# Keys times v left in PSUM for its scan, the first scan in mid-pass, and fourteen list writes a pass in new places on GpSimd's queue

## What is computed

```python
x = x + attn(layernorm(x)); x = x + moe(layernorm(x))

# attn
q, k, v = split(x @ w_qkv);  q, k = elu(q) + 1, elu(k) + 1
running_kv   = scan(k * v, decay)      # s_t = decay * s_(t-1) + x_t, per channel
running_ksum = scan(k, decay)
den = clip(sum(q * running_ksum, per head), 1e-6)
out = (q * running_kv / den) @ w_out

# moe
top_vals, top_idx = top_k(x @ router_w.T + router_b, 4)
rw = softmax(top_vals) * 1.8
routed = sum over the 4 of rw * down_e(silu(gate_e(x)) * up_e(x));  out = routed + shared(x)
```

## Time and profile before

| | us |
|---|---|
| three runs, median (lowest to highest) | 662.66 (661.18 to 666.01) |
| the profiled execution | 662.23 |
| its span, from its first to its last instruction | 660.5 |
| nine steps of the loop, the last of them over at about | 236 |
| 191 tiles, up to about | 596 |

### The profile page before, as it was taken

How to read it: one execution, slowest core, us unless ns; L and a number is a source line. 1 busy time by engine, 2 the same in 40 slices (tenths; PEclk the granted TensorE clock), 3 DMA queues, 4 the chain that set the end, 5 groups by cost and what they waited for, 6 DMA issues and landing times.

```text
span 660.5 us, 15988 instructions
## 1 busy us (share of the span) xinstructions
PE 578.3 (88%) x4909; PEld 409.2 (62%) x4909; DVE 479.9 (73%) x1907; ACT 471.1 (71%) x1138; POOL 438.2 (66%) x359
## 2 busy tenths in 40 slices
PE   4899999899898979999999999999999999998000
PEld 2476676476575557777777777777777777775000
DVE  3569999899979887776666666666666666665163
ACT  4778887769776458897888888788888888787000
POOL 3033177888888877752888888788888788788100
PEclk9999999899999999999999999999999999999555
DMA  8945687879786799976888888898998888886799
GB/s 332 337 147 181 223 261 247 285 265 328 242 265 209 263 288 307 341 265 178 146 141 146 142 143 140 141 147 136 147 146 143 143 140 142 140 140 75 251 409 381
DMA packets 102070, 140.43 MB, mean 213 GB/s; under 512 B 15522, under 2 KB 87746, under 8 KB 101442
## 3 DMA queue, kind: packets, MB, share of 16 engines
q1 hardware_dynamic: 69424, 97.28, 45.9%
q0 software_dynamic: 29040, 38.68, 34.7%
q10 hardware_dynamic: 3522, 3.44, 1.7%
HBM read 79.19 MB, written 64.89 MB: 218 GB/s over the span
## 4 chain that ended last, share of the span: by engine, by line
PE 53%; POOL 13%; DVE 9%; issue 9%; DMA 9%; SPq 3%; ACT 3%; POOLq 0%; ACTq 0%; DVEq 0%
PE psD L1356 13%; PE psQ L1325 12%; PE psK L1325 12%; POOL xlist_scratch L589 8%; PE psT L1296 5%; DMA acc_scratch<-arena 5%; SPq L518 3%; DMA W<-acc_scratch 2%; PE psT L1347 2%; PE psV L1347 2%; PE psD L1413 2%; POOL rstd L574 2%; POOL W L567 1%; POOL acc_scratch L636 1%; DVE stats L843 1%
## 5 line engine op out<-in xcount | busy, mean ns | idle before, releaser
L636 POOL DMA_INDIRECT acc_scratch<-arena x159 | 250.5, 1575 | 72.7 <-ACT arena L692 37.9
L589 POOL DMA_INDIRECT xlist_scratch<-list_row,dest x128 | 136.9, 1069 | 38.6 <-issue 35.9
L1356 PE MATMUL psD<-W,arena 128*128 (+1 forms) x955 | 135.5, 273 | 0.0
L1141 DVE COPY arena<-psT 128x512 f16<-128x512 f16 x191 | 81.0, 424 | 67.2 <-PE psT L1296 65.6
L1325 PE MATMUL psK<-W,arena 128*128 (+1 forms) x576 | 109.3, 326 | 0.7 <-DVE arena L1141 0.7
L1325 PE MATMUL psQ<-W,arena 128*128 (+1 forms) x570 | 108.2, 326 | 0.1
L1356 PEld LDWEIGHTS psD<-W,arena 128*128 128x128 f16 x955 | 85.4, 98 | 6.8 <-ACT arena L680 0.3
L683 ACT ACTIVATE arena<-arena 128x192 f16<-128x192 f32 x191 | 69.2, 362 | 12.0 <-DVE arena L1163 0.6
L692 ACT ACTIVATE arena<-psD,arena 128x256 f32<-128x256 f32 x159 | 73.1, 459 | 6.3 <-DMA acc_scratch<-arena 5.8
L1296 PEld LDWEIGHTS psT<-ident,arena 128*128 128x128 f16 x764 | 58.0, 98 | 25.9 <-issue 2.1
L1296 PE MATMUL psT<-ident,arena 128*128 128x128 f16 x764 | 73.9, 219 | 0.0
(11 more groups left out here) (185 smaller groups left out, 1085.9 us busy)
## 6 DMA issues: line engine op xcount, KB each, us to landing
arena<-xlist_scratch SPq DMA_DIRECT2D x159, 136.0 KB
arena<-in_w_early_dram SPq DMA_DIRECT2D x24, 640.0 KB, 4.9
W<-acc_scratch SPq DMA_DIRECT2D x24, 512.0 KB, 12.6
acc_scratch<-arena SPq DMA_DIRECT2D x16, 512.0 KB, 8.9
arena<-in_L_attn_x_dram SPq DMA_DIRECT2D x10, 512.0 KB, 5.8
xlist_scratch<-pad_scratch SPq DMA_DIRECT2D x32, 136.0 KB
list_row<-xrow_scratch SPq DMA_DIRECT2D x32, 136.0 KB
acc_scratch<-arena SPq DMA_DIRECT2D x33, 128.0 KB, 15.2
```

What stands on the lines that cost most here:

```text
L589: nc.gpsimd.indirect_dma_start(xlist[:, :], bass.IndirectOffsetOnAxis(ap=dest[:, n:n + 1], axis=0), list_row[j % LISTS][:, :], None).then_ ...
L636: nc.gpsimd.indirect_dma_start(acc[t % ACCS][:, :], bass.IndirectOffsetOnAxis(ap=token[:, (t - NT) % DEEP:(t - NT) % DEEP + 1], axis=0), y ...
L1141: nc.vector.tensor_copy(xT[t % 2].rearrange("p s c t -> p (s c t)"), psX[t % 2]).then_inc(xT_done, 1)
L1356: last = nc.tensor.matmul(psY[u], aT[u][0:height, part], weights(t - 2, GUW + q * H, H, height), start=(n == 0), stop=(n == len(parts) - 1))
```

## The change

- DVE's `k_times_v` writes its product back to `psV`, and `kv_sum` scans it from there. PE may write the next v to `psV` only when the scan is done (`kvsum_done` for `kv_done`). ACT may write `kphi` and `kv` of the next sequence earlier.
- `kv_sum(b, 0)` stands right behind `k_sum(b, 0)` in the middle of a step, no longer with `kv_sum(b, 1)` at its end. POOL's product of half 0 follows it and stands apart from that of half 1.
- The ranks are summed in bank 0 of `psD` (the denominators' bank), later in PE's order; `den` waits for `picks_ranked`. `pick`, `count_rows`, `rank_picks` and `sum_ranks` stand in new places on DVE.
- `shift` is one DVE instruction, behind POOL's `root`; the `minus_words` constant, the `less` tile and POOL's instruction go.
- POOL writes 14 lists a step in steps 3 to 8 (15 in steps 3 to 7 and 14 in step 8 before), and 44 instead of 39 behind the loop. In a step it does one list, `root(0)`, six lists, `number_rows`, `root(1)`, product 0, seven lists, product 1.

```diff
-        LIST_FROM = [0, 0, 0] + [15 * n for n in range(NB - 2)] + [89]
+        LIST_FROM = [0, 0, 0] + [14 * n for n in range(NB - 1)]
...
-            return psV if b < NB - 2 else bank_of("rank", 0)
+            return psD[:, 0, :] if b < NB - 2 else bank_of("rank", 0)
...
             def kv_sum_product(b, c):
-                if c == 0:
-                    pool.wait_ge(qphi_done, HC * b + HC)
+                pool.wait_ge(qphi_done, HC * b + c + 1)
...
+                if b >= 3:
+                    list_some(0, 1)
                 if st.after:
                     root(0, b + 1)
                 if b >= 3:
-                    list_some(0, 4)
+                    list_some(1, 7)
...
+                if st.now:
+                    kv_sum_product(b, 0)
                 if b >= 3:
-                    list_some(4, 5)
-                if b >= 3:
-                    list_some(5, 12)
-                if st.now:
-                    kv_sum_product(b, 0)
+                    list_some(7, 20)
+                if st.now:
                     kv_sum_product(b, 1)
-                list_some(12 if b >= 3 else 0, 20)
...
+            def norm_shift(b):
+
+                dve.wait_ge(ln_rstd[0], b + 1)
                 if b >= 1:
-                    dve.wait_ge(ln_shift, b)
-                dve.wait_ge(ln_aggr[0], TS * b + TS)
-                nc.vector.tensor_tensor(less, mv[0][:, :, 0], minus_words[:, :], ALU.mult).then_inc(ln_less, 1)
+                    dve.wait_ge(xn_ready, TS * b)
+                nc.vector.scalar_tensor_tensor(shift, mv[0][:, :, 0], -1.0, rstd[0][:, :], ALU.mult, ALU.mult).then_inc(ln_shift, 1)
...
-                nc.vector.tensor_tensor(kv[c], psV[:, :], kphi[c], ALU.mult).then_inc(kv_done, 1)
...
+                nc.vector.tensor_tensor(psV[:, :], psV[:, :], kphi[c], ALU.mult).then_inc(kv_done, 1)
...
-                nc.vector.tensor_tensor_scan(kvsum[c], decay[:, c:c + 1].to_broadcast([P, S]), kv[c], 0.0, ALU.mult, ALU.add).then_inc(kvsum_done, 1)
+                nc.vector.tensor_tensor_scan(kvsum[c], decay[:, c:c + 1].to_broadcast([P, S]), psV[:, :], 0.0, ALU.mult, ALU.add).then_inc(kvsum_done, 1)
...
                 if st.now:
                     k_sum(b, 0)
+                    kv_sum(b, 0)
...
-                    kv_sum(b, 0)
                     kv_sum(b, 1)
                     clip(b)
```

More of the change, by code:

```diff
@@ L109, in moe_block @@
         rden = carve(TS * HEADS)
-        less = carve(TS)
         shift = carve(TS)
@@ L574, in root @@
                 nc.gpsimd.tensor_tensor(rstd[n][:, :], vare[n][:, :], mhalf[:, :], ALU.pow).then_inc(ln_rstd[n], 1)
[L575 to L578, removed]
             def list_rows(a, z, paced=False):
@@ L940, in k_times_v @@
                 dve.wait_ge(kphi_done, HC * b + c + 1)
-                if not (isinstance(b, int) and b == 0):
-                    dve.wait_ge(attn_done, HC * b)
-                nc.vector.tensor_tensor(kv[c], psV[:, :], kphi[c], ALU.mult).then_inc(kv_done, 1)
+                nc.vector.tensor_tensor(psV[:, :], psV[:, :], kphi[c], ALU.mult).then_inc(kv_done, 1)
             def kv_sum(b, c):
                 dve.wait_ge(kv_done, HC * b + c + 1)
-                nc.vector.tensor_tensor_scan(kvsum[c], decay[:, c:c + 1].to_broadcast([P, S]), kv[c], 0.0, ALU.mult, ALU.add).then_inc(kvsum_done, 1)
+                if b >= 1:
+                    dve.wait_ge(attn_done, HC * b)
+                nc.vector.tensor_tensor_scan(kvsum[c], decay[:, c:c + 1].to_broadcast([P, S]), psV[:, :], 0.0, ALU.mult, ALU.add).then_inc(kvsum_done, 1)
             def attend(b, c):
@@ L999, in step @@
                     norm_stats(1, x1_sb, b - 1)
+                if st.past and st.now:
+                    pick(b - 2)
+                if st.before:
+                    norm_vare(1, b - 1)
+                if st.past and st.now:
+                    count_rows(b - 2)
                 if st.now:
@@ L1004, in step @@
                     nc.vector.tensor_tensor(qks[0], qphi[0], ksum[0], ALU.mult).then_inc(qks_done, 1)
-                if st.before:
-                    norm_vare(1, b - 1)
-                if st.past:
+                if b == NB:
                     rank_picks(b - 2)
-                if b == NB:
+                    sum_ranks(b - 2)
                     place(b - 2)
@@ L1014, in step @@
                     norm(1, xn2, x1_sb, b - 1, xn2_ready)
+                if st.past and st.now:
+                    rank_picks(b - 2)
+                if st.before:
+                    split_rows(b - 1)
+                if st.past and st.now:
+                    sum_ranks(b - 2)
                 if st.now:
                     phi_k(b, 1)
-                if st.before:
-                    split_rows(b - 1)
-                if st.now:
                     k_sum(b, 1)
@@ L1081, in rank_picks, with sum_ranks @@
                                 ALU.mult).then_inc(picks_ranked, 1)
+            def sum_ranks(b):
+                v = nc.vector
                 dve.wait_ge(picks_ranked, b + 1)
@@ L1391, in values @@
             def values(b, c):
-                if c == 1 and b >= 2:
-                    pe.wait_ge(picks_ranked, b - 1)
-                project(psV, b, c, 2, kv_done, v_ready)
+                project(psV, b, c, 2, kvsum_done, v_ready)
             def turn_reciprocals(b):
@@ L1481, in step @@
                     prep_minus_high(b, 4)
+                if st.past and st.now:
+                    rank_rows(b - 2)
+                if st.now:
                     values(b, 1)
@@ L1528, in den @@
                     pe.wait_ge(x1_done, 2 * b)
+                if 2 <= b:
+                    pe.wait_ge(picks_ranked, b - 1)
                 for c in range(HC):
```

32 lines of the change are left out of this document (17 added, 15 removed).

## The result

The changed kernel takes 692.5 us (691.6 to 693.89, four runs) against 663.75 us for the kernel before beside it: ratio 1.0418, 95% interval 1.0371 to 1.0465. The forecast was 679 us, 664 to 686. The direction came out, and so did attend's waits for POOL in steps 4 and 6; the size did not. The profiled execution's span is 689.4 us, 28.9 more than before.

The account below looks back on a forecast made before the run. The prediction took DVE's work (24.05 us) as a full step's floor, with POOL's lateness above it. Steps 2 to 7 gain 14.3 us, step 8 1.0, tiles 2.0, prologue -0.9: 662.23 becomes 678.6, say 679 us, range 664 to 686.

Parts of the forecast that it names:

- products apart: POOL, steps 4 to 7: product 1 alone ends before L852, removing its 1.7 us stall and step 7's 3.45 us wait.
- List rows n = 12, 13 ahead of product 1: POOL's late rows delay product 1, so attend waits 5.9 us in step 4, 5.2 in step 6, some 1.0 in step 8.
- 1.0 us of new idleness on DVE per step: At the clip, which waits for den because one scan covers it instead of two: 1.0 us per step.
- The sum for that step: Step 7's predicted length before small waits: no products wait, clip idleness and late turned reciprocals added, given as 24.9 us.
- Small waits: DVE waits for POOL's roots: shift 1.6 and 1.0 us in steps 3 and 5, norm 0.8 (steps 3 to 6), 1.4 (step 7).
- PE's clock falls as well: Rival, chance 0.13: idle ahead of L1413 lowers PE's clock, up to 3 us more in steps 4 and 6; 685 us.
- The start of the routed tiles: After the loop: the last list write comes 2.4 us nearer the tiles, costing 0 to 2.4 us, taken as 2.0.
- The scan from PSUM: DVE's 14 scans in steps 1 to 7: taken at the same 1.13 us each; bounds -2 to +2.4 us in all.
- the prologue's 0.9: Step 0: moving the shift from POOL to DVE saves 0.9 us.
- step 8: The step after product 1 of step 7: 1.0 us longer (0 to 1.7).
- the rival for "same": Chance 0.15: transfers land in 4 us and small waits vanish (667 us), or only the clip's 1.0 is paid (657).

Follow-up runs that it names:

- lists_behind: The changed kernel with POOL's list writes n = 12, 13 (40, 41; 68, 69) behind product 1 again: ratio 1.0329, 690.0 us.
- early_fetch: The changed kernel with SP fetching rows of already stored shares ahead of the step's own store and padding: ratio 1.0347.
- hold_first: The changed kernel with the last pass's six empty matmuls ahead of den on `psK`, not waiting for the scan: ratio 1.025.
- product0_late: The changed kernel with POOL's product 0 behind the step's list writes, held until `qks` of half 1 is made: ratio 1.0313, 687.4 us.
- change_again: The changed kernel itself, unaltered, once more on another chip: ratio 1.0398 to the kernel before.
- all_and_fetch: The changed kernel with late writes behind product 1, product 0 late, `qks` of half 1 earlier, six empty matmuls on `psK`, early row fetch: ratio 1.0046, 667.95 us.
- before_two: The kernel before with the shift on DVE and both POOL products two list writes earlier: ratio 1.0022.

## Why the forecast was right in direction and short in size

The step that failed is "products apart": product 0 was moved at no price, and it cost 7.0 us of `qks` and 0.9 of the norm. Two more terms were far too small, PE's clock and den in step 7, and the start of the tiles was 4.8 us for 2.0. Of the 13 us between 678.6 and the profiled execution's 691.6, 9.1 lie in steps 2 to 7 (177.09 for 168.0) and 4.7 in the tiles; step 8 gave 1.2 back.

- **"List rows n = 12, 13 ahead of product 1; they wait 5.9 us in step 4, 5.2 in step 6."** The mechanism is shown from both ends. The size was 4.0 and 4.0 of waiting. What failed is mostly the landing: 3.4 and 4.6 us behind the issue in the changed kernel, not 5.07. And the price was smaller than the wait, 0.7 and 1.0 us by `lists_behind`, 1.7 and 2.4 by `early_fetch` (both near what two traces differ by), as long as PE was late for the same attend; with product 0 out of the way it is 3.0 and 2.7.
- **"1.0 us of new idleness on DVE per step" at the clip.** It was 0.93 in steps 3, 4 and 6, and 1.70 and 1.24 in steps 2 and 5, where PE's clock fell and den took 2.69 and 2.23 us for 1.92. In step 7 it was 4.79: I took the step from its turned reciprocals and never followed `psV`, which the change keeps busy through the scan while six empty matmuls ahead of den write it. `hold_first` gives 4.1 us back. (The sum for that step, 26.14 - 3.45 + 1.0 + 1.8 - 0.5, is 25.0 and not 24.9.)
- **"The second alone, 1.26 us, would end long before L852: the 1.7 us stall goes."** It went (-4.8 us). But product 0 I priced at nothing. It moved beside `qks` of half 0, and 7.0 us came there. `qks` took 1.8 us beside product 0 in three steps and 2.60 beside POOL's power and product 0 in two, for 0.69 alone. This is the worst failure, because L852's 1.87 us were in the text, with the reason for them. I applied it to the place the products left and not to the place they went to. The Trainium skill (SBUF — State Buffer, Who interferes with whom) says that a DVE instruction with two SBUF inputs contends with a GpSimd instruction that reads SBUF, through an exclusive lock. The trace agrees with it: `qks` ends 0.55 us behind POOL's instruction. `product0_late` gives 1.9 us back in each of steps 2 and 3, 1.1 and 1.5 against `change_again`.
- **"Small waits": shift 1.6 and 1.0, norm 0.8 to 1.4.** Mostly absent on DVE. In steps 2 to 7 the shift never waited; that attend's waits had moved DVE to a later time would account for it, which no run isolates. The norm waited 1.25 us, in step 7 alone. They made 7.2 us of the sum, so some 6 were wrong in the other direction.
- **"PE's clock falls as well", a rival with 0.13.** It was the case, and in every step, not in steps 4 and 6 alone: I tied it to the waits ahead of L1413 and overlooked that DVE's new delays also stop PE at L1242 and ahead of den. Attend's 5.7 us for the turned reciprocals are its mark, against 1.8 in the sum: 1.74 in step 7, as forecast, and 2.36 and 1.64 in steps 3 and 5, where the sum had nothing.
- **"The start of the routed tiles", 0 to 2.4, taken 2.0.** It was 4.8: the last write came 4.2 us nearer the tiles, not 2.4, and behind the stall the clock is low (0.52 and 0.62), which the bound left out. Another 2 us of the tiles are spread over the routed ones and differ between runs of one structure; their cause stays open.
- The scan from PSUM, the prologue's 0.9 and step 8 (forecast +1.0, measured -0.2) matter little.
- Direction and luck: the rival for "same" asked for transfers that land in 4 us and small waits that vanish, and gave 667. Both came about, nearly (3.4 and 4.6 us; 1.25 of 7.2). By its own terms, with these put right, the forecast would have stood at about 667. That the kernel is slower by 4.2% comes mostly from what the forecast had at nothing or too small: the lock, den in step 7, the clock and the tiles. So the direction was in good part luck.

## What to carry to other kernels

When an instruction moves, ask who its new neighbours are, with the same rule that explained its old ones: a stall that leaves one place may be the same stall in the next. When a buffer is kept longer, list every writer of it, empty matmuls too. And on a loop where three engines are each nearly full, a wait can cost more than itself, since PE may lose its clock behind it (in `all_and_fetch` 1.4 us of a step behind 0.87 us of idleness): price the first idle of PE, not only the waits on the busiest engine.

## What was not expected of the hardware

- PE's granted clock fell to 0.50 behind idle spells as short as 0.87 us (`all_and_fetch`, ahead of den; 0.59 or 0.89 us some 5 us earlier), in every second step, while in the steps between the same spell left it at 1.00.
- The exclusion is not confined to instructions with two tensor inputs. In `change_again`, step 5, the first of the norm's four instructions (one SBUF tensor, its mean and scale from SBUF, f32) starts 0.04 us behind product 0 of POOL and takes 1.36 us; the mean of the line is 0.41 in `product0_late`:

```profile
161.19 1.36 DVE L877 TENSOR_SCALAR W<-arena,mv,rstd 128x256 f32<-128x256 f32 x1 [1.40 <-POOL rstd L571]
```

  The Trainium skill (SBUF — State Buffer, Who interferes with whom) counts `tensor_scalar` among the instructions that can enter a two-port mode and then contend with GpSimd. This agrees with it, though no trace here shows which mode the instruction ran in. The first norm's statistics, one SBUF input, took their usual 1.34 us beside the end of a product in `before_two` (108.32, the products from 106.44 to 109.06).
- On two of the five chips the kernel before took 5 to 6% longer, and the order of two versions turned round: a gain of 0.7% on one chip is a loss of 1% on another. The edited kernels' traces there show PE idle ahead of matmuls of the tiles with nothing seen to end it (25.2 us in 22 idle spells ahead of L1322 in `before_two`, 0.5 us in 3 ahead of the same matmuls, L1336, in the first trace of the change); no trace was kept of the kernel before on these chips, and the cause stays open.
